# The experts' gate in a four-row recurrent block: silu from PSUM on ScalarE, its limit on VectorE, the plus one on ScalarE

## The reference, cut to what matters

```python
p1 = einsum('bsh,eoh->bseo', nf, mlp1_weight) + mlp1_bias      # 8 experts, 2 x 256 outputs
g = jnp.minimum(p1[..., 0::2], 7.0)
lin = jnp.clip(p1[..., 1::2], -7.0, 7.0)
act = g * sigmoid(1.702 * g) * (lin + 1.0)
p2 = einsum('bsei,ehi->bseh', act, mlp2_weight) + mlp2_bias
combined = einsum('bseh,bse->bsh', p2, combine)                # weights of the two chosen experts
out = xc + combined;  s * silu(out) is added to x
```

## Time and profile before

| | |
|---|---|
| three runs | 1730.36, 1734.97, 1735.23 us, median 1734.97 |
| profiled execution, its own time | 1727.02 us |
| its span | 1725.3 us |
| PE, VectorE, ScalarE, GpSimd busy | 1420.9, 1403.6, 1118.5, 984.5 us |
| period of a turn (from the first silu of one's experts to the next's) | 391.3 and 392.8 us |
| experts in the turns | 516.9 to 619.5, 908.2 to 1010.9, 1301.0 to 1403.9 |
| close: first and last 16 rounds | 1468.6 to 1549.6, 1645 to 1712 |

### The profile page before, as it was taken

The page is one execution under the profiler, slowest core; times in us unless marked ns, Lnnn a source line. Parts: engine busy times, 40 slices in busy tenths (PEclk is TensorE's granted clock), DMA queues, the critical chain, the costliest instruction groups (busy, mean ns, idle before and its releaser), DMA issues. The chain is left out here.

```text
span 1725.3 us, 16460 instructions
## 1 busy us (share of the span) xinstructions
PE 1420.9 (82%) x5229; PEld 622.9 (36%) x5296; DVE 1403.6 (81%) x1736; ACT 1118.5 (65%) x1563; POOL 984.5 (57%) x616
## 2 busy tenths in 40 slices
PE   4989989898998879898998789888998763555787
PEld 1444434434443334443443334443443321111333
DVE  2673369999789979999889979989879978999964
ACT  3626678868537768868537768878546854565664
POOL 2143155766208975766307975766406964786675
PEclk8999999999999999999999999999999975686989
DMA  8001000000101000000100100000100300000000
GB/s 191 16 0 61 1 13 1 14 11 1 74 13 37 25 25 1 0 25 0 74 13 20 42 25 1 1 25 1 74 13 0 135 25 0 1 0 1 0 13 13
DMA packets 12600, 42.43 MB, mean 25 GB/s; under 512 B 1866, under 2 KB 1890, under 8 KB 10466
## 3 DMA queue, kind: packets, MB, share of 16 engines
q1 hardware_dynamic: 11698, 35.08, 5.6%
q0 software_dynamic: 816, 6.30, 1.7%
HBM read 38.23 MB, written 4.19 MB: 25 GB/s over the span
## 5 line engine op out<-in xcount | busy, mean ns | idle before, releaser
L772 POOL TENSOR_TENSOR gx<-gx,sy 128x1024 f32<-128x1024 f32 x120 | 293.6, 2447 | 51.3 <-DVE sy L2217 45.0
L795 POOL TENSOR_TENSOR gate<-gate,lin 128x512 f32<-128x512 f32 x120 | 153.0, 1289 | 257.5 <-DVE lin L2337 246.7
L1473 PE MATMUL psf<-g1p,h2w 128*128 128x512 f16 x768 | 178.4, 381 | 2.3 <-ACT tf L965 1.6
L2184 DVE TENSOR_TENSOR psu<-so,psu 128x1024 f32<-128x1024 f32 x128 | 156.7, 1224 | 20.6 <-PE psu L1597 10.6
L1085 ACT ACTIVATE da<-delta,aneg 128x512 f32<-128x512 f32 x256 | 163.9, 712 | 8.0 <-DVE st L2201 7.3
L750 POOL TENSOR_TENSOR g2p<-tf,g2p 128x512 fp32r<-128x512 f32 x64 | 93.8, 1473 | 117.2 <-ACT g2p L988 116.8
L2201 DVE TENSOR_TENSOR_SCAN st<-da,carry,psu 128x512 f32<-128x512 f32 x128 | 156.8, 1267 | 1.8
L2201 DVE TENSOR_TENSOR_SCAN st<-da,psu 128x512 f32<-128x512 f32 x128 | 149.1, 1207 | 1.5
L800 POOL TENSOR_TENSOR ap<-gate,ap 128x512 f16<-128x512 f32 x116 | 143.9, 1258 | 4.4 <-ACT ap L1186 3.7
L2217 DVE TENSOR_TENSOR sy<-st,psu 128x1024 f32<-128x1024 f32 x94 | 114.5, 1218 | 7.9 <-issue 3.5
L1473 PE MATMUL psf<-hp,h1w 128*128 128x512 f16 x512 | 117.4, 379 | 4.3 <-ACT tf L957 4.1
(11 more groups left out here) (395 smaller groups left out, 3383.7 us busy)
## 6 DMA issues: line engine op xcount, KB each, us to landing
mw<-in_mlp_w SPq DMA_DIRECT2D x3, 2048.0 KB, 8.2
xn<-in_x SPq DMA_DIRECT2D x8, 512.0 KB, 5.9
wf<-in_wf SPq DMA_DIRECT2D x4, 1024.0 KB, 4.7
xr<-in_x SPq DMA_DIRECT2D x8, 512.0 KB, 3.9
x<-gx SPq DMA_DIRECT2D x8, 512.0 KB, 3.8
out<-outc SPq DMA_DIRECT2D x8, 512.0 KB, 3.1
mw<-in_mlp_w SPq DMA_DIRECT2D x3, 1024.0 KB, 10.2
h1w<-in_h POOLq DMA_DIRECT2D x1, 2048.0 KB, 13.2
```

The source lines that it names most:

```text
L772: pool.tensor_tensor(out, chunk(gx, c), sy[:, n % 2], ALU.add).then_inc(y_acc.sem, 1)
L795: pool.tensor_tensor(gate[:, r % NG], gate[:, r % NG], lin_at(b, r)[:], ALU.mult)\
L1473: last = pe.matmul(banks[m], w[:, t, cols], src[:, half, t], start=(t == 0 and half == 0), stop=(t == KF - 1 and half == 1))
L2184: dve.tensor_tensor(input_banks(n), chunk(so, c), both(psu[:, row_bank(n)]), ALU.mult)\
```

## The change

`expert_silu` no longer waits for VectorE: it reads the gate's PSUM bank, adds the bias (times 1.702) from a pointer and writes the gate buffer. VectorE's L2326 is gone. Its limit is applied behind the silu, in `expert_scale`, which is now `gate = min(gate, gate_top) * spread` with `gate_top = silu(7 * 1.702)` computed once at the start. The plus one on lin is a new ScalarE operation, `expert_one` (Identity with a bias pointer). `expert_product` waits for it and for the scale. PE's waits that stood on VectorE having emptied the gate bank now stand on the silu, beside the clip's.

Several operations are split into their pieces, so that other work can stand between them: `state_sum` into `state_product` and `state_add`; each `*_root` and `*_std` into `*_log` and `*_root`; `softplus` into three; `expert_sum` into `expert_sum` and `expert_join`; the head's steps into a generator. The instructions in them are the same. The sequences of all four computing engines are written anew; of those, two short stretches are shown, of GpSimd and of ScalarE.

```diff
             def expert_silu(b, r):
-                act.wait_ge(gmin_done.sem, gmin_done.at(b, r + 1))
-                act.activation(gate[:, r % NG], gate[:, r % NG], ACT.Silu, scale=ALPHA)\
-                    .then_inc(sg_done.sem, 1)
+                e, t = divmod(r % NQ, KD)
+                act.wait_ge(p1_mm.sem, p1_mm.at(b, r + 1))
+
+                if r >= NG:
+                    act.wait_ge(alo_done.sem, alo_done.at(b, r - NG + 1))
+                act.activation(gate[:, r % NG], up_bank(b, r)[:, 0], ACT.Silu, scale=ALPHA,
+                               bias=gate_bias[:, e, t:t + 1]).then_inc(sg_done.sem, 1)
+
+            def expert_one(b, r):
+                e, t = divmod(r % NQ, KD)
+                act.wait_ge(lin_done.sem, lin_done.at(b, r + 1))
+                act.activation(lin_at(b, r)[:], lin_at(b, r)[:], ACT.Identity, bias=lin_one[:, e, t:t + 1])\
+                    .then_inc(one_done.sem, 1)
...
+            act.activation(gate_top[:], gate_top[:], ACT.Silu, scale=ALPHA).then_inc(act_const, 1)
...
             def expert_product(b, r):
-                pool.wait_ge(sg_done.sem, sg_done.at(b, r + 1))
+                pool.wait_ge(one_done.sem, one_done.at(b, r + 1))
                 pool.wait_ge(scaled.sem, scaled.at(b, r + 1))
...
                 dve.wait_ge(p1_mm.sem, p1_mm.at(b, r + 1))
-
-                if r >= NG:
-                    dve.wait_ge(alo_done.sem, alo_done.at(b, r - NG + 1))
-                dve.tensor_scalar(gate[:, r % NG], bank[:, 0], mbias[:, e, 0, t:t + 1], LIMIT,
-                                  ALU.add, ALU.min).then_inc(gmin_done.sem, 1)
                 if r >= NL:
                     dve.wait_ge(af_done.sem, af_done.at(b, r - NL + 1))
                 dve.tensor_scalar(lin_at(b, r)[:], bank[:, 1], lin_lo[:, e, t:t + 1], lin_hi[:, e, t:t + 1],
                                   ALU.max, ALU.min).then_inc(lin_done.sem, 1)
 
             def expert_scale(b, r):
-                e, t = divmod(r % NQ, KD)
-                dve.wait_ge(lin_done.sem, lin_done.at(b, r + 1))
+                dve.wait_ge(sg_done.sem, sg_done.at(b, r + 1))
                 dve.wait_ge(cb_mm.sem, cb_mm.at(b, r // KD + 1))
-                dve.scalar_tensor_tensor(lin_at(b, r)[:], lin_at(b, r)[:], lin_one[:, e, t:t + 1],
-                                         spread_bank(b), ALU.add, ALU.mult).then_inc(scaled.sem, 1)
+                dve.scalar_tensor_tensor(gate[:, r % NG], gate[:, r % NG], gate_top[:], spread_bank(b),
+                                         ALU.min, ALU.mult).then_inc(scaled.sem, 1)
...
+            dve.memset(gate_top[:], LIMIT).then_inc(mean_const, 1)
...
+            const(dve.tensor_scalar(gate_bias[:], mbias[:, :, 0], ALPHA, None, ALU.mult))
...
                 else:
+                    pe.wait_ge(sg_done.sem, sg_done.at(b, r - 1))
                     pe.wait_ge(lin_done.sem, lin_done.at(b, r - 1))
...
-                        pe.wait_ge(*((gmin_done.sem, gmin_done.at(b, r)) if half == 0 else
+                        pe.wait_ge(*((sg_done.sem, sg_done.at(b, r)) if half == 0 else
                                      (lin_done.sem, lin_done.at(b, r))))
...
-            def lb_root(b, c, w):
+            def lb_log(b, c, w):
                 act.wait_ge(lb_var.sem, lb_var.at(b, c + 1))
                 root = lb_bank(w)
                 act.activation(root, root, ACT.Ln, bias=eps[:]).then_inc(lb_ln.sem, 1)
+
+            def lb_root(b, c, w):
                 act.wait_ge(lb_ln.sem, lb_ln.at(b, c + 1))
+                root = lb_bank(w)
                 act.activation(root, root, ACT.Exp, scale=-0.5).then_inc(lb_rstd.sem, 1)
...
-            def state_sum(b, c, n):
-                if pooled(b, c * NS + n):
-                    state_product(b, c, n)
-                state_add(b, c, n)
...
-                expert_product(row - 1, 1); expert_product(row - 1, 2); expert_product(row - 1, 3)
-                expert_low(row - 1, 0); expert_low(row - 1, 1); expert_low(row - 1, 2); expert_product(row - 1, 4)
...
+                expert_product(row - 1, 0); expert_product(row - 1, 1); expert_product(row - 1, 2)
+                expert_low(row - 1, 0); expert_product(row - 1, 3); expert_low(row - 1, 1); expert_low(row - 1, 2)
...
+                lb_root(row, 0, wave); expert_one(row - 1, 5); expert_high(row - 1, 4); expert_one(row - 1, 6)
```

More of the change, by code:

```diff
@@ L833, in turn @@
[L833 to L837, removed]
@@ L1305, in turn @@
+                if not last:
+                    l0_root(row + 1, 0)
+                expert_high(row - 1, 30); expert_high(row - 1, 31); decay(row, 0); decay(row, 1)
                 if not last:
                     split_input(row + 1, 0)
-                first_decays(row)
+                decay(row, 2); decay(row, 3)
             def closing(b):
-                expert_gate(b - 1, 1); carry_state(b, 0); expert_square(b, 0); expert_root(b, 0); decay(b, 4)
-                carry_state(b, 1); decay(b, 5); head_square(b, 1); decay(b, 6); c_copy(b, 1); carry_state(b, 2)
@@ new lines, in turn @@
+                state_scan(row - 1, 1, 13); state_output(row - 1, 1, 13); state_input(row - 1, 1, 14)
+                state_scan(row - 1, 1, 14); state_output(row - 1, 1, 14); state_input(row - 1, 1, 15)
+                state_scan(row - 1, 1, 15); state_output(row - 1, 1, 15); run(conv_steps, 18); lf_center(row - 1, 1)
+                run(conv_steps, 28); lf_scale(row - 1, 1); expert_norm(row - 1, 0); expert_weight(row - 1, 0)
+                expert_norm(row - 1, 1); expert_weight(row - 1, 1); run(conv_steps); run(choice, 14); run(weights, 2)
@@ new lines, in turn @@
+                run(conv_steps); run(weights, 7); block_out(row - 1, 0); run(weights); run(conv_steps, 6)
+                run(weights); run(conv_steps, 5); run(weights); run(conv_steps, 4); expert_parts(row - 1, 0)
+                run(conv_steps, 4); expert_parts(row - 1, 1); run(conv_steps, 24); expert_clip(row - 1, 0)
+                expert_clip(row - 1, 1); run(conv_steps); expert_clip(row - 1, 2); expert_scale(row - 1, 0)
+                expert_scale(row - 1, 1); lb_center(row, 0, wave); expert_clip(row - 1, 3); expert_scale(row - 1, 2)
@@ new lines, in turn @@
+                expert_scale(row - 1, 11); expert_scale(row - 1, 12); expert_clip(row - 1, 12)
+                expert_scale(row - 1, 13); expert_clip(row - 1, 13); lb_scale(row, 1, wave); expert_clip(row - 1, 14)
+                head_center(row, 0); expert_clip(row - 1, 15); expert_clip(row - 1, 16); expert_scale(row - 1, 14)
+                expert_scale(row - 1, 15); expert_clip(row - 1, 17); expert_scale(row - 1, 16)
+                expert_scale(row - 1, 17); expert_clip(row - 1, 18); expert_clip(row - 1, 19); run(norm0)
@@ new lines, in turn @@
+                expert_scale(row - 1, 18); expert_scale(row - 1, 19); expert_clip(row - 1, 20); run(norm0)
+                expert_clip(row - 1, 21); expert_sum(row - 1, 0); expert_join(row - 1, 0); expert_scale(row - 1, 20)
+                expert_scale(row - 1, 21); expert_clip(row - 1, 22); head_z0(row, 0); head_z1(row, 0)
+                expert_scale(row - 1, 22); run(parts0, 2); expert_scale(row - 1, 23); run(parts0)
+                expert_clip(row - 1, 23); expert_clip(row - 1, 24); run(parts0, 2); head_softplus(row, 0)
@@ new lines, in closing @@
+                state_input(b, 0, 15); state_scan(b, 0, 15); expert_clip(b, 15); expert_scale(b, 14)
+                expert_scale(b, 15); state_input(b, 1, 0); state_scan(b, 1, 0); state_output(b, 1, 0)
+                state_input(b, 1, 1); state_scan(b, 1, 1); state_input(b, 1, 2); expert_norm(b, 1)
+                expert_weight(b, 1); state_scan(b, 1, 2); run(choice1, 5); state_output(b, 1, 2); state_input(b, 1, 3)
+                run(choice1); lf_center(b, 0); run(choice1, 3); state_scan(b, 1, 3); state_input(b, 1, 4)
```

938 lines of the change are left out of this document (476 added, 462 removed).

## The result

The changed kernel takes 1763.25 us (median of 4 runs, 1762.33 to 1765.73) against 1735.10 (4 runs, 1730.36 to 1735.35): **slower, ratio 1.0171, 95% interval 1.0150 to 1.0192**. The forecast was 1726, the range 1705 to 1744; the rival on the other side said 1742. In the experiments one of the four executions of the new order alone (3347 us) and one with the plus one on VectorE (2612 us, the profiled one) were in a slower state; the times given for these two are medians of the other three.

A forecast was written before the change was run, and what follows sets the result against it. GpSimd was taken to lead the turns' experts, VectorE to bound the close's first rounds, with no engine bounding the whole. Terms -3 - 6 + 1 - 0.7 = -8.7 took 1735.0 to 1726 us, range 1705 to 1744.

The forecast's parts named there:

- What bounds: Turns' experts: GpSimd leads with 91.7 of 100.7 us busy, VectorE 91.2; no engine bounds the whole kernel.
- VectorE's limit: Gate limit, 128 instructions at 0.67 us each: removing it takes 86 us off VectorE's 1403.6 us.
- The plus one: One more ScalarE instruction a round: 712 ns alone, 0.62 us in a row, bounds 0.52 and 0.80.
- A turn's experts, -1 each: Three turns' experts: GpSimd's 3.5 us of fill shrinks by 1 us a turn, between 0 and 3.5; -3 in all.
- The scale's new wait: In expert_scale, now waiting for the silu: VectorE gets 21 us of room in the turns, 10.7 in the close's first rounds.
- The close's first rounds, -6, bounds -10.7 and 0: Close's first 16 rounds: VectorE falls from 74.5 to 63.8 us busy, GpSimd ends 3.5 us lower; -6 taken.
- the last 16 rounds: Close's last 16 rounds: PE's up waits for the silu among table loads, +1 us, range -1 to +4.
- The last chain, -0.7: Last round of the close: without the limit the clip starts at once while ScalarE does the silu, -0.7 us.
- The new sequences, 0: Scans and convolutions: reordering nets 0, -4.9 to +4.9 us a turn; five more table loads, 6.4 us of ScalarE, covered.
- The sum's own range: Whole kernel: 1719 to 1734 us, from the close's bounds (-10.7, 0) and the turns' (-10.5, 0).
- What would show it: Wrong if GpSimd's products wait for the plus one mid-stage, or a turn's period moves over 3 us with the scans' stretch.
- ScalarE's bound: Rival, turns' experts: ScalarE becomes the bound, +4.2 us a turn, +12.6 in all, total 1742; chance 0.28.

## Why the prediction was wrong, point by point

- *What bounds.* GpSimd's lead was read in a stretch that ends with its last products (91.7 beside 91.2 us). In the whole experts of the second turn VectorE has 96.5 and GpSimd 95.6 of 111.1 us: they are level, and which leads is not shown. Wrong is the reading of what a change can do: GpSimd had 15.5 us idle there, and the waits that could enlarge them were looked for in an order that had none.
- *VectorE's limit* (86 us), *the silu* (+0.06 us a round), *the scale* (as before): all three measured as said. *The plus one* at 713 ns against 712. ScalarE's sum for an expert stretch, +21.8: from 82.2 to 104.2 in the second turn, +22.0.
- *A turn's experts, -1 each.* **This step failed.** It measured +9.6, +12.0 and +9.5. The sentence that failed is that both new waits "are covered while ScalarE keeps ahead inside the six gate buffers". For PE's wait the gate buffers are no cover at all: the silu is now what empties the PSUM bank, and of those there are two pairs. Before, VectorE emptied both halves of a bank pair in 1.5 us once it came to them; now half of it waits in a queue with pairs of table loads. The wait alone in the old order costs 84 us, so it is not covered there. Of the 31.1 us in the changed kernel's own experts 14.6 go with the plus one; the other 16.5 stand with no instruction added to ScalarE, and how they divide between PE's wait and the new order is open.
- *The scale's new wait,* for which the prediction gave VectorE's 21 us of room: +35 in the old order in spite of that room. In that trace VectorE's scale waits 118.0 us for the silu, and PE's next spread, which needs the bank that the scale reads, waits 31.1 us for the scale in place of 4.7. In the new order nothing is seen of it.
- *The close's first rounds, -6, bounds -10.7 and 0.* **Wrong too.** From the first silu to the last of these 16 rounds it is 79.4 us before (1469.4 to 1548.8) and 80.1 after (1495.0 to 1575.1), +0.7, though VectorE fell to 65.7 busy, near the 64 that was said. GpSimd, which was to end 3.5 us lower, waits there 9.4 us on its own issue (7.1 before) and 5.8 for plus one and scale (5.1 for the silu before). The scans between the two groups of rounds took 5.0 us more and the last 16 rounds 4.3, where 0 and +1 had been put. Leaving the plus one out shortens the close from 324.0 to 319.7 us; the other 5 us over before are not settled.
- *The last chain, -0.7.* From the end of the last silu to the end it is 18.3 us before and 17.9 after. The term was read wrongly: the product at 1708.98 ran right behind GpSimd's low parts (1706.75, 2.27 us), which is what it waited for, not limit, clip and scale.
- *The new sequences, 0:* -4.4 and -2.8 in scans and convolution, inside the bounds of 4.9. The table loads in the traces are 239 and 246, seven more (9.0 us) and not five: three ahead of the first turn's experts, one behind them, one in the third turn's experts, where none had been put, and two in the close's last rounds. ScalarE's 98.2 us more are the plus one, the silu and the loads (128 x 0.713 + 128 x 0.058 + 9.0 = 107.7 if nothing overlapped), less what neighbours overlap.
- *The sum's own range.* 1719 to 1734 is not what its bounds give. The close (-10.7, 0) and the turns (-10.5, 0) with the other terms as they stand make 1714 to 1735. It changes nothing here, since the time lies outside both.
- *What would show it.* The sign named for being wrong was there: from scan to scan a turn took 399.7 us twice in place of 392.1 and 393.1, and the stretch of scan and convolution was shorter, so the growth is not there. GpSimd's products did wait for the plus one, but little: 3.2, 4.5 and 3.1 us in the three experts.
- *The rivals.* ScalarE's bound had the sign, the stage and the engine, at 1742 with a chance of 0.28. Its 12.6 us for the turns lie near the 14.6 that go there with the plus one, for a reason that did not hold: it priced ScalarE as a full engine (busy time plus unavoidable idle time), and ScalarE was never full: 104 of 123. The other 16.5 us of the turns had no term in any rival. The section of the Trainium skill's page "ScalarE: Activation LUTs" named there, "Rules for kernel authors", was the better guide to the sign: the plus one on ScalarE is 11 to 16 of the 28 us by the run without it. It would not have told of the rest, which has no added ScalarE instruction in it.

What stays open: in the new order, without the plus one and without the scale's wait, 14.5 us over before remain (1747.0 beside 1732.5). PE's wait for the silu is one of the two waits that differ there, and the trace has 5.0 us of it in an expert stretch; but that is a trace of the fastest execution (1737.4), and no run takes this wait away in the new order with the rest kept, so its share is not shown. The order that was laid out to live with it is in the same 14.5 us, and so is whatever PE's lower clock costs (last section).

## What to carry to other kernels

When an operation moves to another engine, ask first what it releases, and count the cover in the buffers of that thing: here two PSUM bank pairs, not six SBUF tiles. An engine with 27% idle time (ScalarE, 73.6 of 100.7 us busy in the earlier trace rows) can still be late for a release, since its queue is in order and holds pairs of table loads; a wait with no work in it cost 84 us in a kernel in which VectorE, ScalarE and GpSimd stayed as busy as they were. To see whether such a wait is covered before the move is made, add the wait alone to the old kernel and run that. It is a price in that order only: an order laid out anew for the move lost 17 us here without the plus one, where the old one lost 103.

## What had not been expected of the hardware

A wait can cost PE twice. In the stretch with the added waits the same matmuls took 98.7 us of PE in place of 89.4, at a granted clock of 0.90 in place of 0.98; in the changed kernel 96.8 at 0.90 beside 90.7 at 0.97. The longer matmuls stand beside pauses of up to 6.4 us between ups. Around the wait of 5.20 us that is shown above, the granted clock was 1.00 (2.4 GHz) while PE ran ahead of it and 0.50 (1.2 GHz) when it took up again, and the four matmuls of an up took 1.89 us in place of 1.03:

```profile
969.00:970.60 1.60, 1.60 (x8) 0.56 (x6) 0.78 (x2) 1.57 (x3) 1.60 (x2) 1.00 0.00 0
975.80:977.80 2.00, 1.96 (x5) 0.69 (x6) 1.50 (x3) 2.00 (x4) 1.42 (x2) 0.50 0.00 0
```

Not every pause is followed by the lower level: in the run with the added waits the up behind one of 2.99 us took 1.04 us. That the pauses are the cause was not tested by itself, nor how much of the 28 us is the clock's.
